# Layer 2's first attention block: divisors spread behind the slot's first turn, the third norm's turn ahead of the products, the next element's values ahead of the last product

## What is computed

```
x = _ln(xx, ln1_g, ln1_b)
x = x + _mha(x, x, a1_..., causal=True)

def _mha(x, y, ...):
    xn = _ln(x, lnx_g, lnx_b);  yn = _ln(y, lny_g, lny_b)
    q, k, v = xn @ wq, yn @ wk, yn @ wv              # per head
    a = softmax(q k^T * D ** -0.5)
    if causal: a = a * (t > s)                       # mask after the softmax
    x_out = x + (a v) @ li1_w + li1_b
    h = gelu(_ln(x_out, ln3_g, ln3_b) @ li2_w + li2_b)
    return x_out + h @ li3_w + li3_b
```

## Time and profile before

| | us |
|---|---|
| runs | 2256.19 (median), 2253.4, 2260.17 |
| profiled execution | 2252.15 |
| its span | 2250.3 |
| VectorE, ScalarE, GpSimd busy in the span | 1335.2, 904.6, 562.6 |
| mean granted clock of TensorE | 0.872 |
| chain that ended last, by engine | PE 68%, DVE 14%, ACT 7%, issue 6%, POOL 4% |

### The profile page before, as it was taken

One profiled execution on the slowest core, in us unless ns is written; L12 is line 12 of the kernel. 1 busy time (PEld: TensorE's weight loads), 2 busy tenths in 40 slices (PEclk: granted clock), 3 DMA queues, 4 the chain that ended last, 5 costly groups with the idle time before them and its releaser, 6 DMA issues.

```text
span 2250.3 us, 57628 instructions
## 1 busy us (share of the span) xinstructions
PE 1991.1 (88%) x22720; PEld 1449.0 (64%) x22720; DVE 1335.2 (59%) x3559; ACT 904.6 (40%) x3432; POOL 562.6 (25%) x1360
## 2 busy tenths in 40 slices
PE   7999999889987998998978788998999999789844
PEld 4899998777566665567866655665654545556623
DVE  6676766765355787545636615886262220678787
ACT  2455554543155664302334523664211111246522
POOL 3566665222011000102335502331000000411111
PEclk9655555999999998999999989999999999889955
DMA  3000001004000001100030000000030000000000
GB/s 135 4 5 5 5 5 43 40 1 187 0 5 8 9 12 70 72 0 24 1 134 5 2 1 8 12 9 2 10 146 0 1 0 4 1 12 14 3 0 17
DMA packets 8025, 56.94 MB, mean 25 GB/s; under 512 B 792, under 2 KB 5248, under 8 KB 5984
## 3 DMA queue, kind: packets, MB, share of 16 engines
q1 hardware_dynamic: 7760, 53.27, 6.1%
HBM read 52.35 MB, written 0.92 MB: 24 GB/s over the span
## 4 chain that ended last, share of the span: by engine, by line
PE 68%; DVE 14%; ACT 7%; issue 6%; POOL 4%; DMA 1%; POOLq 0%; DVEq 0%; SPq 0%; ACTq 0%
PE banks L269 44%; PE banks L274 8%; PE banks L1390 6%; PE banks L963 3%; ACT memory L1011 2%; PE banks L989 2%; DVE memory L1492 2%; PE banks L1543 1%; ACT memory L1417 1%; POOL memory L1449 1%; ACT memory L1424 1%; DVE memory L1498 1%; DVE memory L1273 1%; ACT memory L1256 1%; DVE memory L1501 1%
## 5 line engine op out<-in xcount | busy, mean ns | idle before, releaser
L269 PE MATMUL banks<-memory 128*112 128x256 f32 (+7 forms) x4192 | 1121.4, 423 | 100.7 <-DVE memory L3549 21.5
L269 PEld LDWEIGHTS banks<-memory 128*128 128x128 f32 (+2 forms) x4192 | 699.2, 194 | 431.5 <-issue 276.2
L274 PE MATMUL banks<-memory 112*125 112x112 f32 (+3 forms) x2000 | 301.9, 283 | 76.3 <-DVE memory L850 26.8
L274 PEld LDWEIGHTS banks<-memory 112*125 112x125 f32 (+3 forms) x2000 | 235.9, 171 | 190.3 <-issue 99.8
L1390 PE MATMUL banks<-memory 128*128 128x8 bf16 (+2 forms) x10752 | 306.8, 175 | 14.2 <-DVE memory L1475 1.4
L1390 PEld LDWEIGHTS banks<-memory 128*128 128x128 bf16 x10752 | 295.7, 104 | 25.9 <-POOL memory L1449 23.8
L1011 ACT ACTIVATE memory<-banks,memory 112x375 f32<-112x375 f32 x384 | 215.0, 577 | 25.4 <-DVE memory L1049 25.1
L1049 DVE TENSOR_REDUCE memory<-banks 112x2 f32<-112x750 f32 x192 | 171.0, 933 | 37.3 <-PE banks L963 37.0
L1492 DVE TENSOR_REDUCE memory<-banks 128x48 f32<-128x192 f32 x448 | 121.8, 291 | 62.0 <-PE banks L1390 47.7
L1057 DVE COPY memory<-banks 125x448 f32<-125x448 f32 x192 | 116.8, 618 | 10.7 <-PE banks L274 6.2
L963 PE MATMUL banks<-memory 32*112 32x375 f32 x768 | 88.5, 530 | 19.6 <-ACT memory L1011 17.4
(11 more groups left out here) (240 smaller groups left out, 2436.5 us busy)
## 6 DMA issues: line engine op xcount, KB each, us to landing
memory<-in_l2x SPq DMA_DIRECT2D x1, 7680.0 KB, 21.4
memory<-in_l2f SPq DMA_DIRECT2D x1, 7168.0 KB, 19.4
memory<-in_l1f SPq DMA_DIRECT2D x1, 4617.0 KB, 14.5
memory<-in_ctxT SPq DMA_DIRECT2D x24, 187.5 KB
memory<-in_l2f SPq DMA_DIRECT2D x1, 4096.0 KB, 12.2
memory<-in_l3f SPq DMA_DIRECT2D x1, 3073.0 KB, 22.0
memory<-in_l2a SPq DMA_DIRECT2D x1, 3072.0 KB, 19.5
memory<-in_l0f SPq DMA_DIRECT2D x1, 2304.0 KB, 9.3
```

The source lines that it names most:

```text
L269: ins = self.nc.tensor.matmul(out, weights[i], acts[i], start=i == 0, stop=i == n - 1)
L274: return self.nc.tensor.transpose(out, in_, self.ident[0:n, 0:n])
```

## The change

`order()` can yield "share" behind turned 0 and "inverse" behind turned 2 (`spread_at` = 0) instead of behind all pieces of turned 2 and behind those of turned 3 (`spread_at` = 3, the default). `L2Block1` sets it to 0 and has a new `plan`: "v" of b+1 moves from behind turned 2 to behind norm, ahead of "y"; "xT3" of b-1 moves from behind turned 2 to behind turned 3 and the weights; "xn" of b+2 moves from behind turned 3 to behind "y"; "xT" of b+2 moves from ahead of "y" to behind "xn".

```diff
--- before.py
+++ after.py
@@ -1158,6 +1158,7 @@
 
     nk = S
     keep = None
+    spread_at = 3
 
     def __init__(self, k):
         super().__init__(k)
@@ -1184,15 +1185,21 @@
             pieces = [[(kind, b + ahead, i) for kind, i, ahead in gap if 0 <= b + ahead < B] for gap in self.plan]
             for r in range(3):
                 yield "turned", b, r
+                if r == self.spread_at:
+                    yield "share", b, 0
+                elif r == self.spread_at + 2:
+                    yield "inverse", b, 0
                 yield from pieces[r]
-            yield "share", b, 0
+            if self.spread_at == 3:
+                yield "share", b, 0
             if b + 1 < B:
                 yield "all", b + 1, 0
             yield "turned", b, 3
             for r in range(4 if b + 1 < B else 0):
                 yield "weights", b + 1, r
             yield from pieces[3]
-            yield "inverse", b, 0
+            if self.spread_at == 3:
+                yield "inverse", b, 0
             yield "products", b, 0
             yield "norm", b, 0
             yield from pieces[4]
@@ -2383,11 +2390,12 @@
 
 class L2Block1(L2Block, TiledSelf):
     k_pieces, key_step, v_by_act = 1, 4, (0,)
+    spread_at = 0
     lib, ln, ln3 = 4, 0, 8
     prologue = (("ln", 0, 1), ("xT", 0), ("xm", 0), ("xm", 0, 1), ("k", 0), ("q", 0), ("stats", 0, 1), ("xn", 0, 1))
     second = (("v", 0, 0), ("xT", 0, 1))
     plan = ((("k", 0, 1), ("xn3", 0, -1), ("ln", 0, 2)), (("q", 0, 1), ("xm", 0, 2)),
-            (("v", 0, 1), ("xT3", 0, -1), ("stats", 0, 2)), (("xn", 0, 2),), (("xT", 0, 2), ("y", 0, 0), ("stats3", 0, 0)))
+            (("stats", 0, 2),), (("xT3", 0, -1),), (("v", 0, 1), ("y", 0, 0), ("xn", 0, 2), ("xT", 0, 2), ("stats3", 0, 0)))
     tail = (("xn3", 0), ("xT3", 0))
 
     def __init__(self, k):
```

## The result

The changed kernel takes 2279.2 us (2276.6 to 2282.4, 4 runs) against 2254.8 us of before: 1.0107 times as long, 95% interval 1.0093 to 1.0121, +24.4 us. Forecast were +14.6 us and 2270.8 us, the latter from before's first three runs, whose median was 2256.2 us. The range of 2256 to 2284 us held. Run again beside the experiments the ratio was 1.0093 (1.0078 to 1.0108), about +21 us. The stage itself, from its first transposes to the first matmul of the next stage, went from 143.7 us (1162.70 to 1306.42) to 164.4 us (1166.82 to 1331.19): +20.7 us. The profiled span grew by 28.9 us, but 4.1 us of that lie ahead of the stage and 4.1 behind it, where the program is the same; the profiled execution of before, 2252.2 us, was faster than all four of its timed runs. The spans of all experiments less their stage are 2109 to 2116 us, against 2106.6 us of before.

What follows compares the result with a forecast made beforehand. TensorE, busy 88% of the span, was taken as the bound, its waits in layer 2's first attention block as what could move. +11.3 us at equal clock plus +3.3 us for clock gave +14.6 us, 2270.8 us; range 2256 to 2284.

Steps and rivals of the forecast that it cites:

- The ring: One slot as a cycle of step distances from R, start of an element's four score reductions, to the next R.
- R to v: From the start of the score reductions: v waits for reductions and xT3's bank read, starting no sooner than 2.80 us.
- R to R about 17.4 us at clock 1.00: Sign of being right: one period, between successive elements' score reduction starts, takes about 17.4 us at full clock.
- One wait on v's bank takes the place of the three: TensorE's waits of 1.28, 1.26 and 0.35 us are replaced by v's bank wait; -0.14 us up to y.
- six periods, equal clock: Six stretches between successive score reduction starts, clock effects left out: 1.2 + 10.0 + 1.5 us longer.
- clock in these periods: One fall to TensorE's lower clock in each of six periods instead of four, 1.65 us each: +3.3 us.
- behind the last R: Tail after the last score reductions start: last products come at 1295.1 against 1296.26 us, -1.2 us.
- rival 3: Two clock falls a slot, behind the products' wait and behind y: +24.5 us, 2280.7 us; chance 0.13.
- Rival 1: Same ring, but TensorE's clock better than now: 2258 to 2266 us, say 2262; chance 0.20.
- rival 4: v covers L1291 and neither its bank nor xT's read holds TensorE: -16 us, 2240 us; chance 0.11.
- Rival 2: L850 behind y not stretched by GpSimd, 0.41 us in each inner period: +12.0 us, 2268.2 us; chance 0.12.
- rival 5: Moved steps land where the old waits were; nothing changes beyond noise: 2256 us; chance 0.06.

Runs made afterwards that it cites:

- e3: Changed kernel with the products' 16 matmuls and turned 0's four transposes each issued three times, filling TensorE's waits: 2264.5 us, 1.0033 of before.
- e4: Changed kernel with GpSimd's add held until VectorE's L850 of xn is done: 2267.0 us, 1.0034 of before.
- e12: Changed kernel with only the products issued three times, turned 0 once: 2269.1 us, 1.0043 of before.
- e5: Kernel before the change with the products' 16 matmuls issued twice: 2247.5 us, 0.9960 of before.
- e1: Kernel before with only the early share and inverse, old plan kept: 2255.1 us, 0.9981 of before.
- e11: Changed kernel run once more with no edit: 2280.9 us, 1.0093 of before.

## Why the prediction was right in sign and short in size

The ring was right, step by step, to within 0.16 us. Beside the prediction's distances stand those of e3_after_filled, where the clock stays at 1.00 (R at 1241.39 and 1258.94):

| step | predicted us | measured us |
|---|---|---|
| R to v | 2.80 | 2.96 |
| v to the read of y | 3.71 | 3.77 |
| read of y, L850, to xT | 1.45 (L850 0.93) | 1.43 (L850 0.91) |
| xT to k | 1.84 | 1.80 |
| k to q | 2.18 | 2.26 |
| q to R | 5.38 | 5.33 |
| period | 17.4 | 17.55 |

The prediction's sign "R to R about 17.4 us at clock 1.00" is seen only there: no period of the changed kernel itself is at 1.00. "One wait on v's bank takes the place of the three" holds: the longest wait of a slot is that for L2337. L850 was stretched by its neighbour to within 0.02 us of the pattern. Here page and row part again: by the Trainium skill (SBUF — State Buffer, section Who interferes with whom) the one that issues first holds the shared port pair, but L850 starts 0.04 us ahead of L2386 in the profile and is still the one that is stretched; and e4_add_late shows that the neighbour is the cause, since without it L850 takes 0.41 us. Whether the start in the profile tells which of the two issued first is not shown.

The sum, term by term. For the measured terms the six periods of the changed kernel at full clock are taken from fills that don't lengthen the ring: 16.8 (e3), four times 17.55 (e3) and 16.0 (e12), 103.0 us; those of before from e5: five times 14.88 and 14.31, 88.7 us.

| term | predicted us | measured us |
|---|---|---|
| six periods, equal clock | +12.7 | 103.0 - 88.7 = +14.3 |
| clock in these periods | +3.3 | (119.9 - 103.0) - (95.3 - 88.7) = +10.3 |
| behind the last R | -1.2 | 18.7 - 22.3 = -3.6 |
| ahead of R(1) | -0.2 | -0.4 |
| stage | +14.6 | +20.7 |

Of the 6.1 us by which the stage's forecast was short, 7.0 are the clock in the periods and 1.6 the ring; the tail gave 2.4 back.

**The term that was mis-sized is the clock's**, "one fall in each of the six periods instead of four: 2 x 1.65". The count was too low and so was the price. The trace has eight falls: in v and y in five periods, in k (and q) in three. The clock takes 119.9 - 103.0 = 16.9 us of the changed kernel's six periods, and 11.4 of them lie in two (23.28 and 23.24 less 17.55 each). In these both things happen that rival 3 had for every period, a fall behind v's wait and another behind y's waits:

```profile
1274.76 6.46 PE L269 MATMUL banks<-memory 128*112 128x512 f32 x12 [2.35 <-DVE memory L2337]
1282.75 0.80 PE L274 MATMUL banks<-memory 112*128 112x112 f32 x6 [1.53 <-DVE memory L850]
1284.55 3.76 PE L269 MATMUL banks<-memory 128*128 128x112 f32 x16 [1.01 <-DVE memory L2337]
```

v and y take 6.46 us here instead of 3.67, and k 3.76 instead of 2.04. From v to k this slot takes 2.8 us more than e3's, and from k to R 2.9 us more: all that these falls slow (v, y, k and q) lies on the ring. The other four falls, one to a period, cost 0.9 to 1.7 us (17.74 less 16.8; 18.98 and 19.23 less 17.55; 17.43 less 16.0), about the 1.65 us of the forecast or less, though three of them slow v and y together. So the price holds for a fall that is alone in its period and is too low where two come close together; why those are dearer is not shown. The Trainium skill (TensorE: Matmul & The Clock Gate, section HAM oscillation — how this bites in real kernels), cited for rival 3, speaks of waits for DMAs; the waits for other engines here bring the lower level again and again too, and with the waits filled 16.9 us of loss become 1.6 (e3) and 3.3 (e12), and before's 6.6 become none (e5). But four of the six periods have one fall only, so rival 3 as priced for all periods (+24.5) was too much for the stage (+20.7). That the median moved by +24.4 us is no mark for it. The median lies in the upper part of the forecast's range, the part that was there because of rival 3.

In the tail the clock helped: y of the last slot takes 1.98 us (1325.50) instead of 3.75, and so the tail was 3.6 us shorter, not 1.2. The ring's part was even a little less than forecast: the last products start at R + 11.32 (1323.79), where the prediction had R + 10.95 and before R + 12.12. The rest is mostly the clock's.

Rival 1 (a better clock) and rival 4 (three waits won) fall; e1 shows that even without the new plan TensorE's waits shrink by only 0.35 of the 2.9 us in an inner slot, and the period by 0.2. Rival 2 falls by L850's 0.91 us, and rival 5 (nothing beyond the noise) by the time. Of the +24.4 us between the medians of the first comparison the stage has 20.7; e11's +21 us leaves almost nothing over and the two intervals overlap, so the other 3.7 us are not shown to be of the change. Why the falls come where they do is not settled: e4 moved them with 0.5 us, and nothing here says beforehand which slot gets one.

## What to carry to other kernels

A wait that goes is won only as far as the next-latest step allows: write the slot as a ring of distances, walk the PSUM banks in their new order, and look at what stands ahead of each bank's reader in its own queue. A step that is moved behind the last matmul of a slot puts its whole norm, turn and read on the ring. Price a fall of TensorE's clock by the work on the ring behind the wait, and leave room for two falls that come close together: here they cost 5.7 us in one period, a fall alone 0.9 to 1.7. Where a wait can't be removed, matmuls that repeat finished work into the same bank can be worth their time, as in e3 and e5.

## What the runs showed of the hardware that I had not expected

- Added work made two kernels faster: e5 with 16 more matmul calls a slot by 0.40%, e3 against the changed kernel by 15 us.
- The falls of the clock are the same in two executions of one program (periods equal to 0.03 us), yet in the trace of e4 a change of 0.5 us in a slot went with three periods without any.
- VectorE's L850 takes 0.41 us alone, 0.60 beside the end of a mask, 0.91 beside GpSimd's 0.72 us add and 1.19 beside its 0.98 us mask, though by the profile it starts first in the last two.
